# Wide causal attention: k and v projected as two pieces in the third and fourth slot of a unit, and a mask product of 256 columns

## The chip, the cores and the metric

The kernel runs on one core of one Trainium2 chip. The core has a matrix engine (TensorE, in the profile PE, its weight loads PEld), a vector engine (VectorE, DVE), a scalar engine (ScalarE, ACT), GpSimd (POOL) and SyncE (SP), which here issues the transfers. TensorE writes to PSUM, eight banks of 512 float columns; the other operands lie in SBUF. The metric is the device time of one execution in microseconds, as the median of several runs.

## The reference

Four transformer layers on x of 8 sequences x 256 positions x 256 channels. The change touches one of them, the attention of the third layer:

```python
B, T, E = (2, 256, 256)      # the batch is 8 in this case
G, QPG, D = (4, 4, 128)
q = (x @ wq + bq).reshape(b, t, G, QPG, D).transpose(0, 2, 3, 1, 4)
kv = (x @ wkv + bkv).reshape(b, t, G, 1, 2 * D).transpose(0, 2, 3, 1, 4)
k, v = (kv[..., :D], kv[..., D:])
q = q + pe
k = k + pe
scores = jnp.einsum('bgqtd,bgksd->bgqts', q, k) / math.sqrt(D)
causal = jnp.tril(jnp.ones((t, t), dtype=bool))
scores = jnp.where(causal, scores, -jnp.inf)
probs = jax.nn.softmax(scores, axis=-1)
out = jnp.einsum('bgqts,bgksd->btgqd', probs, v).reshape(b, t, G * QPG * D)
return out @ wo
```

x is normalised before it and the result is added to x. pe is a sinusoidal position table. Four heads of a group share one k and one v.

## The kernel before

`four_layers_kernel` runs stages one after the other with a barrier between them: per layer an attention and a feed-forward stage. The function `wide_attention_stage` serves the third layer (`WideAttention(4, 4, shared_kv=True, rope=False, causal=True, ...)`) and the fourth (`rope=True`, not causal). For the fourth, the change alters nothing in what is computed or in its order; the branches with `rope` stay.

All of it works in float32 accuracy from pairs: a number is split into a high part and the rest (low), and each product is made of three passes (high-high, high-low, low-high).

The work is cut into units. A unit is one group of four heads and one sequence, so there are 4 x 8 = 32 units (`over_units`), written out by hand at the edges of a group and as a loop in its middle. A unit has four slots, one for each head (`over_slots`). In slot j of unit u TensorE does, in this order:

- `value` of the head before (L661): out^T = v^T probs^T, 6 products;
- the piece for this slot of the *next* unit: a projection of the normalised x (L583);
- `transposed` of head j (L646): three transposes of the probabilities, after ScalarE's exponentials (`probs_ready`);
- `score` of the next head (L627 and L636): the mask product and six products q^T k;
- `output` of the head before (L583, bank<-w,out_t): six products with wo.

Which slot has which piece stands in `self.pieces` and `self.after` (L306 to L308): q (heads 0 and 1) in slot 0, q2 (heads 2 and 3) in slot 1, kv in slot 2, nothing in slot 3. q and q2 take 12 products of 256 columns each. kv takes 6 of 256 for k and 12 of 128 for v (`bank<-w,z`), and fills one bank: k in its first half, v in its second.

A piece is then read from its bank by VectorE, which adds bias and position (L791, L796) into a buffer `summed`; ScalarE copies that as the high part (L706), and GpSimd subtracts to make the low part (L871, `sum_low`). The scores of the next unit's first head, in slot 3, wait for all three low parts (L620).

Between the transposes of head j and those of head j + 1 the other engines work on the probabilities in turn: ScalarE copies the transposed ones (L732), VectorE subtracts for their low part (L816), then takes the maximum of the next head's scores (L807) and the reciprocal (L829), and ScalarE makes the next exponentials (L724). VectorE and ScalarE take their operations strictly in the order of the program; VectorE's order in a slot is: low part of the output of the head before (L821), the piece's additions, L816, L807, L829, and the addition of the result to x (L835).

The mask is added by TensorE too: before the scores an identity is multiplied with `masks_bf`, 128 x 384 in bfloat16: the triangle for the first 128 queries, zeros for the first half of the second 128 queries' keys, and the triangle for their second half. It opens the bank (`start=True`); the score products accumulate on it. The first 128 queries see 128 keys only, so the scores take 128 + 256 = 384 columns.

Each group has its own weights, in two buffers (high and low). The weights of the next group are split in the slots of the last units of a group (`split_parts_at`, L514): q's in slot 2 and k's and v's in slot 3 of the unit before the last, those of the output in slot 1 of the new group's first unit.

Of the kernel before, what the change touches and what calls it, by code (L numbers as in the profile page):

```python
# [30 lines left out]
P = 128  # L31
# [237 lines left out]
    return slice(t * S, (t + 1) * S)  # L269


def make_masks(nc, masks_bf, mask):

    nc.vector.memset(masks_bf[:, P:2 * P], 0.0)
    nc.vector.tensor_copy(masks_bf[:, 0:P], mask[:])
    return nc.vector.tensor_copy(masks_bf[:, 2 * P:3 * P], mask[:])


class WideAttention:
# [7 lines left out]
    def __init__(self, heads, groups, shared_kv, rope, causal, scale):  # L287
        self.HG, self.G, self.rope, self.causal, self.scale = heads, groups, rope, causal, scale
        self.shared_kv, self.KV = shared_kv, 1 if shared_kv else heads
        widths = [2 * P, heads * P, self.KV * P, self.KV * P] if rope else [heads * P, P, P]  # L290
        scales = [1.0, scale, 1.0, 1.0] if rope else [scale, 1.0, 1.0]
        names = ["rope", "q", "k", "v"] if rope else ["q", "k", "v"]
        at, self.segment, self.parts = 0, {}, []
        for name, width, s in zip(names, widths, scales):
            self.segment[name] = (len(self.parts), at, width)
            self.parts.append((at, at + KT * width, s))
            at += KT * width
        self.wo_at, self.width = at, at + heads * C
        self.parts.append((at, self.width, 1.0))

        if rope:
            self.pieces = [("q", False, ["q"]), ("k", False, ["k"]), ("v", False, ["v"]), ("rope", True, ["rope"])]
            self.before = {0: [0], 1: [2]}
            self.after = {0: [1], 1: [3]}
        else:
            self.pieces = [("q", True, ["q"]), ("q2", True, ["q"]), ("kv", True, ["k", "v"])]  # L306
            self.before = {}
            self.after = {0: [0], 1: [1], 2: [2]}  # L308
        self.ahead = 1 if rope else 0
        self.sums = [i for i, p in enumerate(self.pieces) if p[1]]  # L310


def wide_attention_stage(core, cfg, w_in, consts_in):
# [15 lines left out]
    with Stage(core) as st:  # L329
# [5 lines left out]
        if rope:  # L335
            tables = st.sb("tables", [P, 2, 2 * S])
            consts = [tables]
            turned = st.sb("turned", [P, 2, 2 * S])
            summed = [st.sb("summed", [P, 2 * S]) for _ in range(2)]
            halves = st.sb("halves", [P, 2, 2, S], F32R)  # L340


            q_turned = [st.sb("q_turned", [P, 2, S], F32R) for _ in range(2)]
            k_turned = [[st.sb("k_turned", [P, 2, S], F32R) for _ in range(2)] for _ in range(2)]
            zeroed = st.sem("zeroed")
            moved = [st.sem("moved") for _ in range(2)]
            halves_high, halves_low = st.sem("halves_high"), st.sem("halves_low")
            MOVES = 8
        else:
            position = st.sb("position", [P, S])  # L350
            bias = st.sb("bias", [P, G, HG + 1])
            v_bias = st.sb("v_bias", [P, G, P])
            mask = st.sb("mask", [P, P])
            consts = [position, bias, v_bias, mask]
            scaled_position = st.sb("scaled_position", [P, S])
            scaled_bias = st.sb("scaled_bias", [P, G, HG])
            masks_bf = st.sb("masks_bf", [P, S + P], BF16)
            summed = [st.sb("summed", [P, 2 * S]) for _ in range(2)]
        probs = [st.sb("probs", [P, QT, S]) for _ in range(2)]
        probs_t = [[st.sb("probs_t", [P, NB], F32R) for _ in range(2)] for _ in range(2)]  # L360
# [116 lines left out]
        def destination(u, i, part):  # L477

            name = cfg.pieces[i][0]
            if name == "q":  # L480
                return [(q[u.parity][part][:, 0:2, :], slice(0, 2 * S))]
            if name == "q2":
                return [(q[u.parity][part][:, 2:4, :], slice(0, 2 * S))]
            if name == "k":
                return [(k[u.parity][part][:, 0:2, :], slice(0, 2 * S))]
            if name == "v":
                return [(v[u.parity][part][:], slice(0, 2 * S))]
            return [(k[u.parity][part][:, 0, :], slice(0, S)), (v[u.parity][part][:], slice(S, 2 * S))]

        def shaped(source, target):  # L490
            return source.rearrange("p (a c) -> p a c", a=target.shape[1]) if len(target.shape) == 3 else source
# [13 lines left out]
        def wait_weights_free(eng, g, part):  # L505

            if part < NW - 1:

                last = part if rope else (2 if part == 0 else 3)
                need(eng, piece_done, (g * B - 1) * NP + AHEAD + last)  # L510
            else:
                need(eng, y_done, g * B * HG)

        def split_parts_at(u, j):  # L514

            if not u.in_last_group:
                if u.next().closes:
                    parts = ({0: [0], 1: [1, 2]} if rope else {2: [0], 3: [1, 2]}).get(j, [])
                    return u.g + 1, parts
                if rope and u.closes and j == 0:  # L520
                    return u.g + 1, [3]
            if u.opens and not u.first and j == 1:
                return u.g, [NW - 1]
            return None, []
# [4 lines left out]
        with nc.Block() as block:  # L529
# [40 lines left out]
            def _(pe):  # L570
# [16 lines left out]
                def piece(u, i):  # L587
# [10 lines left out]
                    zz = z[u.parity]  # L598
                    if name != "v":
                        s = segments[0]  # L600
                        for c in range(1 if name == "kv" else 2):
                            first = (c + (2 if name == "q2" else 0)) * P
                            ins = group_of_passes(p[:, c * S:(c + 1) * S], [
                                (lambda a, kt=kt: weights(a, s, kt, first, P), lambda c_, kt=kt: norm_t[c_][:, kt, bass.ds(u.b * S, S)])
                                for kt in range(KT)])
                    if "v" in segments:
                        at = S if name == "kv" else 0
                        for t in range(QT):
                            ins = group_of_passes(p[:, at + t * KV * P:at + (t + 1) * KV * P], [
                                (lambda a, kt=kt: zz[a][:, kt, t * P:(t + 1) * P],  # L610
                                 lambda c_, kt=kt: weights(c_, "v", kt, 0, KV * P)) for kt in range(KT)])
                    ins.then_inc(piece_done, 1)

                def score(u, j):
                    if j == 0:
                        if rope:
                            pe.wait_ge(piece_read, piece_number(u, 1))
                            wait_moved(pe, u)
                        else:
                            pe.wait_ge(sum_low, (u.n + 1) * NS)  # L620
                    if rope and u.first and j == 0:
                        pe.wait_ge(zeroed, 4)
                    need(pe, probs_ready, u.slot(j) - 1)
                    s = s_bank[j % 2]
                    qq, kk, kj = q[u.parity], k[u.parity], 0 if cfg.shared_kv else j
                    if causal:
                        nc.tensor.matmul(s[:, 0:S + P], core.ident_bf[:], masks_bf[:], start=True, stop=False)  # L627
                    for t in range(QT):
                        width = P if causal and t == 0 else S
                        operands = [(qq[a][:, j, t * P:(t + 1) * P], kk[c][:, kj, 0:width])  # L630
# [3 lines left out]
                                         for a, c in ((0, 0), (0, 1), (1, 0))]  # L634
                        for n, (a, c) in enumerate(operands):
                            ins = nc.tensor.matmul(s[:, score_columns(causal, t)], a, c, start=(n == 0 and not causal),  # L636
                                                   stop=(n == len(operands) - 1 and (t == QT - 1 or not causal)))
                    ins.then_inc(scores_done, 1)

                def transposed(u, j):  # L640
# [9 lines left out]
                def value(u, j):  # L650
# [2 lines left out]
                    need(pe, o_low, m)  # L653
                    if j == 0 and rope:
                        pe.wait_ge(piece_read, piece_number(u, 2))
                    jv, vv, pp = 0 if cfg.shared_kv else j, v[u.parity], probs_t[j % 2]
                    for kt in range(QT):
                        to = slice(P, S) if causal and kt else slice(0, S)
# [84 lines left out]
            def _(dve):  # L743
# [23 lines left out]
                def piece(u, i):  # L767
# [17 lines left out]
                        ins.then_inc(piece_read, 1)  # L785
                        return
                    need(dve, sum_low, number - 1)
                    for c in range(1 if name == "kv" else 2):
                        head = c + (2 if name == "q2" else 0)
                        b_ap = bias[:, bass.ds(u.g, 1), HG:HG + 1] if name == "kv" else scaled_bias[:, bass.ds(u.g, 1), head:head + 1]  # L790
                        ins = nc.vector.scalar_tensor_tensor(  # L791
                            target[:, c * S:(c + 1) * S], p[:, c * S:(c + 1) * S], b_ap.rearrange("p a c -> p (a c)"),
                            (position if name == "kv" else scaled_position)[:], ALU.add, ALU.add)
                    if name == "kv":
                        b_ap = v_bias[:, bass.ds(u.g, 1), :].to_broadcast([P, QT, P])
                        ins = nc.vector.tensor_tensor(target[:, S:2 * S].rearrange("p (a c) -> p a c", a=QT),  # L796
                                                      p[:, S:2 * S].rearrange("p (a c) -> p a c", a=QT), b_ap, ALU.add)
                    ins.then_inc(piece_read, 1)

                def score(u, j):  # L800
# [1916 lines left out]
```

## Time and profile before

| | us |
|---|---|
| median of 3 runs | 3215.28 (3204.89 to 3218.27) |
| the profiled execution's own time | 3212.33 |
| its span, first to last instruction | 3210.3 |
| TensorE busy | 2779.6 (87%) |
| VectorE busy | 2066.0 (64%) |
| ScalarE busy | 1601.6 (50%) |
| GpSimd busy | 734.5 (23%) |

The mean granted clock of TensorE over the span is 0.934. The stage that the change touches lies from about 1143 to 1680 us; its first scores start at 1154.09. In a timeline row the columns are start, busy time, engine, line, operation, output and inputs, their shape and the number of instructions merged; a mark in brackets gives the idle time of the engine just before and whose work ended it. Busy times of products overlap, as TensorE is pipelined: what a product costs in a row of them is read from one start to the next.

### The profile page before, as it was taken

The page shows a single profiled execution, that of the slowest core. Times are in us where ns is not written, and L with a number is a line of the kernel's source. Part 1 is how long each engine was busy: PE and PEld are TensorE (multiplying, and loading weights), DVE is VectorE, ACT ScalarE, POOL GpSimd, SP SyncE. Part 2 cuts the span into 40 slices and gives each one's busy share as a digit, 9 for nine tenths or more (in the row PEclk, how much of TensorE's full clock was granted, in tenths as well). Part 3 has the DMA queues.
Part 4 walks back from the last instruction along what each step waited for, and adds up shares of the span by engine and source line. Part 5 has one row for each costly group of instructions (what it writes and reads, how often), then busy time and mean ns, then how long its engine had stood idle before and what let it go on. Part 6 is the DMA issues. An engine that isn't in the chain of part 4 may idle for free. (4 is left out here: it accounts for less than half of the span.)

```text
span 3210.3 us, 67512 instructions
## 1 busy us (share of the span) xinstructions
PE 2779.6 (87%) x20975; PEld 2421.0 (75%) x20979; DVE 2066.0 (64%) x6053; ACT 1601.6 (50%) x4675; POOL 734.5 (23%) x676
## 2 busy tenths in 40 slices
PE   6976999799996579999986879999999996949995
PEld 5755888566665379989984669999999995637774
DVE  5666555677783477777774367777777777425554
ACT  6872333599995155555554444444454444113331
POOL 2110000111100222222224511010101101756663
PEclk9987999899998589999997979999999997969998
DMA  4001111460001020110003533333332325557776
GB/s 127 2 9 35 51 46 51 166 231 2 2 2 41 0 79 27 57 45 33 34 17 135 171 120 94 88 102 100 102 97 86 98 86 216 196 146 122 123 123 163
DMA packets 177282, 274.93 MB, mean 86 GB/s; under 512 B 28016, under 2 KB 145704, under 8 KB 173712
## 3 DMA queue, kind: packets, MB, share of 16 engines
q1 hardware_dynamic: 150352, 228.13, 22.3%
q0 software_dynamic: 26688, 43.80, 6.9%
q8 instruction: 125, 2.05, 0.3%
q14 instruction: 117, 0.96, 0.1%
HBM read 106.97 MB, written 80.98 MB: 59 GB/s over the span
## 5 line engine op out<-in xcount | busy, mean ns | idle before, releaser
L583 PE MATMUL bank<-norm_t_high,w 128*128 128x256 f32 (+1 forms) x2176 | 448.6, 288 | 8.3 <-DVE w L758 8.3
L724 ACT ACTIVATE probs<-bank,neg_max 128x256 f32<-128x256 f32 (+1 forms) x512 | 224.5, 443 | 367.3 <-DVE inv L829 357.6
L583 PEld LDWEIGHTS bank<-norm_t_high,w 128*128 128x128 f32 x2176 | 364.8, 195 | 9.1 <-issue 9.1
L1143 ACT ACTIVATE probs<-neg_scores,bound 128x256 f32<-128x256 f32 (+1 forms) x768 | 367.0, 487 | 2.4 <-DVE bound L1214 1.9
L583 PE MATMUL bank<-norm_t_low,w 128*128 128x256 f32 (+1 forms) x1088 | 310.8, 286 | 0.0
L1214 DVE CUSTOM_DVE_ANT_0 neg_scores<-bank,table 128x256 f32<-128x256 f32 (+1 forms) x768 | 261.8, 397 | 58.6 <-PE bank L1055 58.6
L636 PE MATMUL bank<-k,q 128*128 128x256 f32 (+1 forms) x1536 | 270.8, 299 | 7.5 <-DMA k_turned<-halves 6.3
L732 ACT ACTIVATE probs_t<-bank 128x384 fp32r<-128x384 f32 (+1 forms) x256 | 139.3, 544 | 261.4 <-PE bank L646 260.7
L865 POOL TENSOR_TENSOR summed<-turned 128x512 f32<-128x512 f32 x64 | 82.5, 1289 | 707.1 <-DVE turned L784 707.1
L835 DVE SCALAR_TENSOR_TENSOR x_sb<-bank,inv,x_sb 128x256 f32 (+1 forms) x512 | 224.3, 479 | 24.3 <-DVE inv L829 13.4
L583 PE MATMUL bank<-w,out_t 128*128 128x256 f32 x1536 | 226.7, 283 | 4.3 <-DVE out_t L821 4.1
L2205 POOL DMA_INDIRECT sums<-shared,norm_t x127 | 197.3, 1553 | 132.8 <-ACT shared L2033 128.8
L661 PE MATMUL bank<-probs_t,v 128*128 128x256 f32 (+1 forms) x1536 | 216.8, 277 | 4.5 <-issue 2.9
L636 PEld LDWEIGHTS bank<-k,q 128*128 128x128 f32 x1536 | 212.2, 191 | 11.2 <-issue 9.7
L2018 ACT ACTIVATE acted<-bank 128x176 f32<-128x176 f32 (+2 forms) x222 | 69.5, 313 | 297.9 <-PE bank L1971 218.1
L583 PEld LDWEIGHTS bank<-norm_t_low,w 128*128 128x128 f32 x1088 | 212.0, 195 | 0.0
L1971 PE MATMUL bank<-weights,x_t 128*128 x696 | 208.0, 422 | 3.4 <-issue 1.3
L583 PEld LDWEIGHTS bank<-w,out_t 128*128 128x128 f32 x1536 | 201.7, 190 | 6.6 <-DVE out_t L821 4.4
L661 PEld LDWEIGHTS bank<-probs_t,v 128*128 128x128 f32 x1536 | 200.2, 191 | 6.6 <-DVE probs_t L816 3.5
L1067 PE MATMUL bank<-ident_sb,probs 128*128 128x128 f32 x1408 | 192.7, 278 | 12.8 <-ACT probs_t L1150 12.7
L1067 PEld LDWEIGHTS bank<-ident_sb,probs 128*128 128x128 f32 x1408 | 155.0, 141 | 58.1 <-issue 29.5
L1222 DVE COPY probs_t<-bank 128x512 f32<-128x512 f32 (+1 forms) x192 | 123.5, 643 | 77.7 <-PE bank L1067 76.6
(371 smaller groups left out, 6697.1 us busy)
## 6 DMA issues: line engine op xcount, KB each, us to landing
z<-norm_t_high SPq DMA_DIRECT2D x96, 256.0 KB, 2.5
z<-norm_t_low SPq DMA_DIRECT2D x96, 256.0 KB, 2.5
rows<-blank SPq DMA_DIRECT2D x1, 21336.0 KB, 65.6
norm_t<-rows SPq DMA_DIRECT2D x127, 168.0 KB, 2.9
q_turned<-halves SPq DMA_DIRECT2D x256, 64.0 KB, 2.0
k_turned<-halves SPq DMA_DIRECT2D x256, 64.0 KB, 2.0
staged<-in_attention SPq DMA_DIRECT2D x12, 1280.0 KB, 6.6
staged<-in_experts SPq DMA_DIRECT2D x34, 448.0 KB
```

The costliest lines, as they stand in the source:

```text
L583: ins = nc.tensor.matmul(out, stationary(a), moving(c), start=(kt == 0 and m == 0), stop=(kt == n - 1 and m == 2))
L636: ins = nc.tensor.matmul(s[:, score_columns(causal, t)], a, c, start=(n == 0 and not causal), stop=(n == len(operands) - 1 and (t == QT - ...
L661: ins = nc.tensor.matmul(o_bank[:, to], vv[a][:, kt, jv * P:(jv + 1) * P], pp[c][:, of], start=(kt == 0 and n == 0), stop=(kt == QT - 1 an ...
L724: ins = nc.scalar.activation(probs[j % 2][:, t, 0:width], s_bank[j % 2][:, score_columns(causal, t)], ACT.Exp, bias=neg_max[j % 2][:, t:t ...
L732: nc.scalar.activation(probs_t[j % 2][0][:], t_bank[:, 0:NB], ACT.Copy).then_inc(t_high, 1)
L835: ins = nc.vector.scalar_tensor_tensor(tile, y_bank[j % 2][:, t * C:(t + 1) * C], inv[j % 2][:, t:t + 1], tile, ALU.mult, ALU.add)
L1067: ins = nc.tensor.transpose(t_bank[g % 2][:, at:at + P], probs[q % 2][g][:, t, kt * P:(kt + 1) * P], core.ident[:])
L1143: ins = nc.scalar.activation(probs[q % 2][g][:, t, 0:width], neg_scores[g][:, t, 0:width], ACT.Exp, bias=bound[q % 2][:, g, t:t + 1], scal ...
L1214: ins = nc.vector.tensor_tensor_reduce(out=neg_scores[g][:, t, 0:width], in0=s_bank[g][:, t * S:t * S + width], in1=table[:, at:at + width ...
L1222: nc.vector.tensor_copy(probs_t[q % 2][g][:], t_bank[1][:, 0:NB]).then_inc(t_by_dve, 1)
L1971: ins = nc.tensor.matmul(out, x_t[i.e % 2][:, kt, :], weights[:, kt * i.columns:][:, bass.ds(expert[i.e], i.columns)], start=(kt == 0), st ...
L2205: nc.gpsimd.indirect_dma_start(scratch.results[e % len(scratch.results)], bass.IndirectOffsetOnAxis(ids, 0), product[e % OUT_RING], None, ...
```

## The change

1. The piece kv becomes two pieces, k in slot 2 and v in slot 3. There are four pieces in a unit instead of three (NP and NS), each with its own bank turn, `summed` buffer, semaphore counts and waits. The scores of the next unit's first head wait for the low parts of q, q2 and k alone (`u.n * NS + 3`); a new wait for all four stands before the `value` of each unit's first head.
2. The split of v's weights for the next group moves from slot 3 of the unit before the last to slot 0 of the last unit; k's stays in slot 3.
3. `masks_bf` is 128 x 2 x 128 without the zeros, and the mask product writes columns 0 to 127 and 256 to 383 of the bank. Columns 128 to 255 are first written by the score product of the second 128 queries, which accumulates in a bank that the mask product has opened.

```diff
+def mask_product(nc, core, s, masks_bf):
+    diagonal = s[:].rearrange("p (a c) -> p a c", a=2)[:, :, 0:P]
+    return nc.tensor.matmul(diagonal, core.ident_bf[:], masks_bf[:], start=True, stop=False, skip_group_check=True)
+
 def make_masks(nc, masks_bf, mask):
-    nc.vector.memset(masks_bf[:, P:2 * P], 0.0)
-    nc.vector.tensor_copy(masks_bf[:, 0:P], mask[:])
-    return nc.vector.tensor_copy(masks_bf[:, 2 * P:3 * P], mask[:])
+    nc.vector.tensor_copy(masks_bf[:, 0, :], mask[:])
+    return nc.vector.tensor_copy(masks_bf[:, 1, :], mask[:])
...
-            self.pieces = [("q", True, ["q"]), ("q2", True, ["q"]), ("kv", True, ["k", "v"])]
-            self.after = {0: [0], 1: [1], 2: [2]}
+            self.pieces = [("q", True, ["q"]), ("q2", True, ["q"]), ("k", True, ["k"]), ("v", True, ["v"])]
+            self.after = {0: [0], 1: [1], 2: [2], 3: [3]}
...
-                last = part if rope else (2 if part == 0 else 3)
+                last = part if rope else part + 2
...
-                    parts = ({0: [0], 1: [1, 2]} if rope else {2: [0], 3: [1, 2]}).get(j, [])
+                    parts = ({0: [0], 1: [1, 2]} if rope else {2: [0], 3: [1]}).get(j, [])
                     return u.g + 1, parts
-                if rope and u.closes and j == 0:
-                    return u.g + 1, [3]
+                if u.closes and j == 0:
+                    return u.g + 1, [3 if rope else 2]
...
-                            pe.wait_ge(sum_low, (u.n + 1) * NS)
+                            pe.wait_ge(sum_low, u.n * NS + 3)
...
-                        nc.tensor.matmul(s[:, 0:S + P], core.ident_bf[:], masks_bf[:], start=True, stop=False)
+                        mask_product(nc, core, s, masks_bf)
...
+                    elif j == 0:
+                        pe.wait_ge(sum_low, (u.n + 1) * NS)
```

On TensorE, in slots 2 and 3 of a unit, the rows stand in this order before (`w,z` is v's product, `norm_t_high,w` and `norm_t_low,w` are k's):

```order
L583 MATMUL bank<-norm_t_high,w 128x256
L583 MATMUL bank<-w,z 128x128 x12
L646 MATMUL bank<-ident_sb,probs 128x128 x3
L627 MATMUL bank<-masks_bf,ident_bf 128x384
L636 MATMUL bank<-k,q 128x128 x3
L636 MATMUL bank<-k,q 128x256 x3
L583 MATMUL bank<-w,out_t 128x256 x6
L661 MATMUL bank<-probs_t,v 128x256 x3
L661 MATMUL bank<-probs_t,v 128x128 x3
L646 MATMUL bank<-ident_sb,probs 128x128 x3
```

and with the change:

```order
L587 MATMUL bank<-norm_t_high,w 128x256
L650 MATMUL bank<-ident_sb,probs 128x128 x3
L276 MATMUL bank<-masks_bf,ident_bf 128x2x128
L639 MATMUL bank<-k,q 128x128 x3
L639 MATMUL bank<-k,q 128x256 x3
L587 MATMUL bank<-w,out_t 128x256 x6
L667 MATMUL bank<-probs_t,v 128x256 x3
L667 MATMUL bank<-probs_t,v 128x128 x3
L587 MATMUL bank<-w,z 128x128 x12
L650 MATMUL bank<-ident_sb,probs 128x128 x3
```

v's twelve products have moved from before the first group of transposes to before the second.

On VectorE, the same place before (L791 with `bias` is k's addition, L796 v's):

```order
L821 TENSOR_TENSOR out_t<-bank,out_t 128x256
L791 SCALAR_TENSOR_TENSOR summed<-bank,bias,position 128x256
L796 TENSOR_TENSOR summed<-bank,v_bias 128x256
L816 TENSOR_TENSOR probs_t<-bank,probs_t 128x384
L807 TENSOR_REDUCE neg_max<-bank 128x1 x2
L829 RECIPROCAL inv<-sums 128x2
L835 SCALAR_TENSOR_TENSOR x_sb<-bank,inv,x_sb 128x256 x2
L821 TENSOR_TENSOR out_t<-bank,out_t 128x256
L816 TENSOR_TENSOR probs_t<-bank,probs_t 128x384
```

and with the change:

```order
L831 TENSOR_TENSOR out_t<-bank,out_t 128x256
L799 SCALAR_TENSOR_TENSOR summed<-bank,bias,position 128x256
L826 TENSOR_TENSOR probs_t<-bank,probs_t 128x384
L817 TENSOR_REDUCE neg_max<-bank 128x1 x2
L839 RECIPROCAL inv<-sums 128x2
L845 SCALAR_TENSOR_TENSOR x_sb<-bank,inv,x_sb 128x256 x2
L831 TENSOR_TENSOR out_t<-bank,out_t 128x256
L796 TENSOR_TENSOR summed<-bank,v_bias 128x256
L826 TENSOR_TENSOR probs_t<-bank,probs_t 128x384
```

v's addition has moved one slot on, to the place that the other pieces' additions have in theirs.

## Rows read from the trace of the kernel before

**Rows 1.** Busy time by engine in a window; then clock, DMA share, GB/s.
```profile
1158.00:1674.30 516.30, 488.77 (x4080) 479.07 (x4078) 394.56 (x1084) 281.90 (x898) 123.92 (x124) 1.00 0.11 36
```
**Rows 2.** Waits from 1150 to 1685 us: in total, times, longest.
```profile
PE bank L646 <- ACT probs L724: 21.2, 35, 0.7
```
**Rows 3.** Timeline of TensorE, one unit; columns as above.
```profile
1270.46 0.49 PE L646 MATMUL bank<-ident_sb,probs 128*128 128x128 f32 x3
...
1274.48 0.49 PE L646 MATMUL bank<-ident_sb,probs 128*128 128x128 f32 x3
...
1277.01 0.34 PE L583 MATMUL bank<-norm_t_high,w 128*128 128x256 f32 x1
...
1277.77 1.45 PE L583 MATMUL bank<-w,z 128*128 128x128 f32 x12
1279.06 0.52 PE L646 MATMUL bank<-ident_sb,probs 128*128 128x128 f32 x3
...
1282.37 0.55 PE L646 MATMUL bank<-ident_sb,probs 128*128 128x128 f32 x3 [0.60 <-ACT probs L724]
...
1286.43 0.49 PE L646 MATMUL bank<-ident_sb,probs 128*128 128x128 f32 x3
```
**Rows 4.** Timeline of TensorE and VectorE in the last unit.
```profile
1667.11 0.55 PE L646 MATMUL bank<-ident_sb,probs 128*128 128x128 f32 x3 [0.60 <-ACT probs L724]
...
1670.45 0.55 PE L646 MATMUL bank<-ident_sb,probs 128*128 128x128 f32 x3 [0.59 <-ACT probs L724]
...
1671.56 0.56 DVE L816 TENSOR_TENSOR probs_t<-bank,probs_t 128x384 fp32r<-128x384 f32 x1 [0.43 <-ACT probs_t L732]
```
**Rows 5.** Timeline of all engines between two groups of transposes.
```profile
1279.44 0.98 PE L636 MATMUL bank<-k,q 128*128 128x128 f32 x6
...
1280.13 0.56 DVE L816 TENSOR_TENSOR probs_t<-bank,probs_t 128x384 fp32r<-128x384 f32 x1
...
1280.61 0.61 DVE L807 TENSOR_REDUCE neg_max<-bank 128x1 f32<-128x128 f32 x2
...
1280.99 0.74 POOL L871 TENSOR_TENSOR k<-summed,k 128x256 fp32r<-128x256 f32 x1 [3.33 <-ACT v L706]
...
1282.12 0.20 ACT L724 ACTIVATION_READ_ACCUMULATOR probs<-bank,neg_max 128x1 f32 x1
1282.21 0.38 ACT L737 ACTIVATE out_t<-bank 128x256 fp32r<-128x256 f32 x1
```
**Rows 6.** Weight loads behind a mask product: two windows, from 1274.82 and 1275.1.
```profile
1274.81 0.46 PEld L636 LDWEIGHTS bank<-k,q 128*128 128x128 f32 x3
...
1274.97 0.41 PEld L636 LDWEIGHTS bank<-k,q 128*128 128x128 f32 x3
```
**Rows 7.** Timeline where the next group's weights are split.
```profile
1260.58 1.05 ACT L686 ACTIVATE w<-staged 128x1024 fp32r<-128x1024 f32 x1
...
1262.04 0.51 PE L646 MATMUL bank<-ident_sb,probs 128*128 128x128 f32 x3
...
1263.54 0.42 DVE L796 TENSOR_TENSOR summed<-bank,v_bias 128x256 f32<-128x256 f32 x1
1263.87 0.55 DVE L816 TENSOR_TENSOR probs_t<-bank,probs_t 128x384 fp32r<-128x384 f32 x1
...
1266.10 0.55 PE L646 MATMUL bank<-ident_sb,probs 128*128 128x128 f32 x3 [0.72 <-ACT probs L724]
```
**Rows 8.** Timeline of a group's first unit, slot 2 of it.
```profile
1290.46 0.49 PE L646 MATMUL bank<-ident_sb,probs 128*128 128x128 f32 x3
...
1296.44 0.51 PE L646 MATMUL bank<-ident_sb,probs 128*128 128x128 f32 x3
```
**Rows 9.** Timeline of the stage's start.
```profile
1150.59 1.26 POOL L871 TENSOR_TENSOR q<-summed,q 128x512 fp32r<-128x512 f32 x1 [0.79 <-ACT q L706]
...
1154.09 0.34 PE L627 MATMUL bank<-masks_bf,ident_bf 128*128 128x384 bf16 x1 [3.15 <-POOL v L871]
```
**Rows 10.** Timeline of TensorE, the stage's one stop with no releaser.
```profile
1417.54 1.29 PE L661 MATMUL bank<-probs_t,v 128*128 128x256 f32 x6 [2.88 <-issue]
```

More of the change, by code:

```diff
@@ L356, in wide_attention_stage @@
             scaled_bias = st.sb("scaled_bias", [P, G, HG])
-            masks_bf = st.sb("masks_bf", [P, S + P], BF16)
+            masks_bf = st.sb("masks_bf", [P, 2, P], BF16)
             summed = [st.sb("summed", [P, 2 * S]) for _ in range(2)]
@@ L484, in destination @@
             if name == "k":
[L485 to L488, printed above, removed]
+                return [(k[u.parity][part][:], slice(0, KV * S))]
+            return [(v[u.parity][part][:], slice(0, KV * S))]
         def shaped(source, target):
@@ L600, in piece @@
                         s = segments[0]
-                        for c in range(1 if name == "kv" else 2):
+                        for c in range(KV if name == "k" else 2):
                             first = (c + (2 if name == "q2" else 0)) * P
@@ L606, in piece @@
                     if "v" in segments:
-                        at = S if name == "kv" else 0
                         for t in range(QT):
-                            ins = group_of_passes(p[:, at + t * KV * P:at + (t + 1) * KV * P], [
+                            ins = group_of_passes(p[:, t * KV * P:(t + 1) * KV * P], [
                                 (lambda a, kt=kt: zz[a][:, kt, t * P:(t + 1) * P],
@@ L636, in score @@
                             ins = nc.tensor.matmul(s[:, score_columns(causal, t)], a, c, start=(n == 0 and not causal),
-                                                   stop=(n == len(operands) - 1 and (t == QT - 1 or not causal)))
+                                                   stop=(n == len(operands) - 1 and (t == QT - 1 or not causal)),
+                                                   skip_group_check=causal)
                     ins.then_inc(scores_done, 1)
@@ L787, in piece @@
                     need(dve, sum_low, number - 1)
-                    for c in range(1 if name == "kv" else 2):
-                        head = c + (2 if name == "q2" else 0)
-                        b_ap = bias[:, bass.ds(u.g, 1), HG:HG + 1] if name == "kv" else scaled_bias[:, bass.ds(u.g, 1), head:head + 1]
-                        ins = nc.vector.scalar_tensor_tensor(
[L792 to L797, printed above, removed]
+                    if name == "v":
+                        b_ap = v_bias[:, bass.ds(u.g, 1), :].to_broadcast([P, QT, P])
+                        ins = nc.vector.tensor_tensor(target[:, 0:S].rearrange("p (a c) -> p a c", a=QT),
+                                                      p[:, 0:S].rearrange("p (a c) -> p a c", a=QT), b_ap, ALU.add)
+                    elif name == "k":
+                        ins = nc.vector.scalar_tensor_tensor(
+                            target[:, 0:S], p[:, 0:S], bias[:, bass.ds(u.g, 1), HG:HG + 1].rearrange("p a c -> p (a c)"), position[:], ALU.add, ALU.add)
+                    else:
+                        for c in range(2):
+                            head = c + (2 if name == "q2" else 0)
+                            b_ap = scaled_bias[:, bass.ds(u.g, 1), head:head + 1]
+                            ins = nc.vector.scalar_tensor_tensor(
+                                target[:, c * S:(c + 1) * S], p[:, c * S:(c + 1) * S], b_ap.rearrange("p a c -> p (a c)"), scaled_position[:],
+                                ALU.add, ALU.add)
                     ins.then_inc(piece_read, 1)
```

## The prediction

> **What bounds the kernel now.** I read the page first (the table above): its busy shares are means over many stages, and the change touches one of them. So the next view is the table of windows for that stage, the wide causal attention of the third layer (1158 to 1674.3 us). There TensorE is busy 488.77 of 516.30 us at a granted clock of 1.00, the upper of its two levels, 2.4 GHz; VectorE is busy 394.56 us and nobody else comes near [rows 1]. So TensorE is the bound, with 27.5 us in which it is idle. The list of waits says where: 21.2 us in 35 pieces are transposes (L646) that wait for ScalarE's exponentials (L724) [rows 2]. 35 is nearly one for each of the 32 units.
>
> The timeline of TensorE in one unit shows which slot waits. I measure a slot from the first transpose of a head to that of the next [rows 3]. Slot A (from 1270.46) holds the product of piece q2 and lasts 4.02 us; B (from 1274.48) holds kv and lasts 4.58; C (from 1279.06) holds no piece and lasts 3.31; D (from 1282.37) holds the next unit's q and lasts 4.06. The sum is 15.97. Only C's end carries the idle mark (0.60 us, on the exponentials).
>
> What ends C is a chain through three engines, seen in the timeline of all engines [rows 5]: transposes at 1279.06, ScalarE's copy of them, VectorE's subtraction 1280.13, the maximum of the next head's scores 1280.61, exponentials read out by 1282.12 + 0.20, and the next transposes at 1282.37, 0.05 later. That is 3.31 us whatever TensorE does in between. The last unit, which has no pieces at all, runs every slot on this chain: 1667.11 to 1670.45 is 3.34 [rows 4]. So a slot costs the larger of TensorE's own work and about 3.31 to 3.34.
>
> **The change part by part.**
>
> 1. Slot B loses v's product. v's 12 products of 128 columns stand from 1277.77 to the transposes at 1279.06, which is 1.29 us (0.108 each) [rows 3]. TensorE's work in B falls from 4.58 to 3.29, or 3.24 with the smaller mask product (point 3). That is now just under the chain, so the chain ends B: 3.31. Gain 1.27. TensorE then idles under 0.1 us here; the cover for a longer chain is gone in this slot.
>
> 2. Slot C gains v's product. What a slot holds beside its piece is read from B: 1274.48 to 1277.01, 2.53 us [rows 3]. C becomes 2.53 + 1.29, less 0.05 for the mask, plus about 0.03 because v now follows other 128-column products: 3.80. That is 0.5 over the chain, so the 0.60 idle goes and nothing waits in its place. Loss 0.49.
>
> 3. The mask product goes from 384 to 256 columns, 128 times. Its price is not its duration but how long it holds up the next weight load. The first load behind it starts at 1274.81, and three loads are still seen from 1274.97 on [rows 6]: a gap of 0.16 us, where 128-column products follow one another every 0.108 and 256-column ones every 0.12 (six of them from 1277.01 to 1277.77, with a start of 0.17) [rows 3]. 256 columns of the mask should cost 0.11. Gain 0.05 in each slot that TensorE bounds (A, C, D), nothing in B, where the chain decides. Bounds: 0 if the gapped target (two runs of 128 columns) costs what was saved, 0.06 at best. I take 0.05. No row shows a product with such a target.
>
> 4. D begins after a stop now and runs 0.04 longer than A, the time in which the loads start up again. Without the stop, D is 4.02 and with the mask 3.97: gain 0.09. A: 4.02 to 3.97, gain 0.05.
>
> In one unit: 1.27 - 0.49 + 0.09 + 0.05 = 0.92. Pieces are made in 31 of the 32 units: 31 x 0.92 = 28.5 us.
>
> The Trainium skill (TensorE: Matmul & The Clock Gate, Back-to-back issue gap) gives about 81 ns for sustained 128-column products with their weight loads; the trace disagrees with 108 [rows 3]. By the page v's product would be 0.97 and C 3.48, and the gain 31 x 0.32 = 9.9 us larger. The trace is of this very product, so the sum keeps 1.29.
>
> 5. Work of the other engines: the number and size of VectorE's, ScalarE's and GpSimd's operations is the same, half of what stood in slot B moves on to C. In B and C VectorE has the same order (piece, subtraction, maximum), and both slots' ends now have what slots A and D have already: one piece between value and transpose. At B's end the chain runs through q2's additions, as it does before; at C's end it is longer at most by VectorE's k addition, under 0.5 us of cover.
>
> 6. Waits that are new. The scores of the next unit's first head (in C) now wait for q, q2 and k only, and the values of that head, one slot later, for v. k's rest on GpSimd starts 1.93 us after the transposes that open C and takes 0.74 [rows 5]; with v no longer in front of it on ScalarE it ends no later than 2.7. The scores stand behind v's product and three transposes, 3.80 + 0.33 after the same point. 1.4 us are left. v's rest has a whole slot more. Behind those scores stand the output and value products, on which everything waits, so if this were late it would count in full; it isn't by these rows. SP's loads of the inputs of v wait for the pieces of two units back, as before, and v reads them a slot later: more room.
>
> 7. Where a group of heads ends, weights are split. Once in each of three groups the split of q's 1024 columns (ScalarE, 1.05 us from 1260.58) makes slot C 4.06 instead of 3.31 (1262.04 to 1266.10) [rows 7]. Here the chain decides, and it starts at the split, 5.52 us before 1266.10; v's product hid its first 1.46 us. In the change slot C opens 0.16 after the operation that follows the exponentials on ScalarE (1282.21 to 1282.37) [rows 5], which here is the split. So C is 5.52 - 0.16, less 0.33 for v's addition (1263.54 to 1263.87), which leaves VectorE's queue there: 5.03. B + C was 4.59 + 4.06 (B by the trace of this unit as in the others) and becomes 3.31 + 5.03; D, with one small split fewer, falls from 4.36 (1266.10 to 1270.46) to 3.97 [rows 3, 7]; the unit gains 0.31 + 0.39 + 0.05 = 0.75 instead of 0.92: 3 x -0.17 = -0.5. In the first unit of three groups slot B lasts 5.98 (1290.46 to 1296.44) [rows 8], for the split of the output weights; it loses v's 1.29 and the mask's 0.05 and would be 4.64, but the split lies on the chain too, so I take 4.8, a gain of 1.2 instead of 1.27: -0.2.
>
> 8. The stage's start. TensorE's first scores stood idle for 3.15 us until 1154.09, for GpSimd's rests of q2 (1.26 from 1150.59), k and v [rows 9]. Now k can follow q2 at once at 1151.85, ends 0.74 later at 1152.6, and v is not waited for: 1.5 us earlier. Bounds 0.7 (v's operation alone, as long as k's) and the whole 3.15.
>
> Sum: 28.5 - 0.5 - 0.2 + 1.5 = 29.3 us. Against the profiled execution's own time, 3212.33 us, that gives 3183.0; the median of the runs shown is 3 us above the profiled one, so I predict 3184.
>
> **Rivals.**
> - The filled slot is right, but the mask product saves nothing (the gapped target costs what the columns save): 3 x 31 x 0.05 = 4.7 less, 3189. For it: no such product in the trace. Against: the array takes the same stream of columns.
> - Slot B's chain is longer than read, since what B was hiding (output and value products, VectorE's reads of x) now runs close behind it. 3.31 and 3.34 are the two readings; if VectorE's addition of k came on top (at 0.33, as v's in [rows 7]), B would be 3.64: 31 x 0.33 = 10 less, 3194. Against: VectorE's subtraction started 1.07 after the transposes where kv's additions stood before it (1280.13), and 1.11 in the last unit, where none did (1671.56) [rows 4, 5].
> - The gap comes back as stalls of another kind. Once, before 1417.54, TensorE stands 2.88 us for nothing that the profile shows, and its six products behind it take 1.29 [rows 10], where six steps of 0.12 and an end would be 0.8: some 3.4 us in all. The loops' code changes in length; one such stall more in each of eight turns of a loop gives 3184 + 27 = 3211, no change.
> - Slower than before: the mask product with two runs of 128 columns. If such a target kept the next weight load from starting before the product has ended, each would cost the full duration of a short product, 0.27 us (three transposes take 0.49, less two steps of 0.11), and a load step of 0.11 [rows 3]: 0.38. Slots A, C and D pay it whole, B only what is over the 0.2 us by which the scores' end (1279.44 + 0.98) lies ahead of their maximum (1280.61) [rows 5]. It decides from 0.28 us each; at 0.38 it costs 96 x 0.38 + 32 x 0.18 = 42 us and the 4.7 saved: 3231. For it only that no row shows such a target. Against: the stream into the array is one of 256 columns either way, and the steps of 0.12 in [rows 3] are the same whichever part of a bank a product writes.
>
> **How the numbers follow.** Forecast 0.80 (its own range 3175 to 3193, from 0 or 0.06 for the mask, 0.7 or 3.15 at the start, and the 13 us between the runs shown); mask saves nothing 0.07; longer chain 0.05; stalls 0.05; gapped target 0.03. The range reaches over the first two rivals: 3172 to 3198. A difference of 0.5% is 16 us: faster 0.92, same 0.05, slower 0.03.
>
> **What the profile would show.** The transposes' wait for the exponentials falls from 21.2 us to a few, in pieces under 0.1 us, and stands at the end of slot B. Slots of one unit read 3.97, 3.31, 3.80, 3.97 and sum to 15.05. The weight load behind the mask product starts 0.11 after the one before. The stage takes about 29 us less and everything behind it starts as much earlier with unchanged lengths. I am wrong if B stays above 3.5, if C shows an idle mark, or if the scores wait for GpSimd's k inside the units.

## The result, and the profile after

| | before | with the change |
|---|---|---|
| median, us | 3216.23 (6 runs) | 3192.65 (3183.33 to 3196.18, 6 runs) |
| the profiled execution, us | 3212.33 | 3183.33 |
| ratio, 95% interval | | 0.9922 [0.9904, 0.9939] |
| steady unit: slots A, B, C, D; the unit (medians) | 4.00, 4.58, 3.31, 4.06; 15.96 | 3.98, 3.29, 3.88, 3.99; 15.13 |

By the medians the change makes the kernel 23.6 us faster. On a second chip, on which the kernel before took 3299.55 us, it took 3272.07 us, a ratio of 0.9917 [0.9904, 0.9929]. The profiled execution with the change is the fastest of its six. A steady unit is one that lies at no edge of a group of heads, where weights are split.

The first view is again the timeline of TensorE in one unit, with the change:

```profile
1261.64 0.49 PE L650 MATMUL bank<-ident_sb,probs 128*128 128x128 f32 x3
...
1265.59 0.49 PE L650 MATMUL bank<-ident_sb,probs 128*128 128x128 f32 x3
...
1268.88 0.55 PE L650 MATMUL bank<-ident_sb,probs 128*128 128x128 f32 x3
...
1271.42 1.50 PE L587 MATMUL bank<-w,z 128*128 128x128 f32 x12
1272.76 0.51 PE L650 MATMUL bank<-ident_sb,probs 128*128 128x128 f32 x3
...
1276.74 0.49 PE L650 MATMUL bank<-ident_sb,probs 128*128 128x128 f32 x3
```

Against [rows 3]: B has fallen from 4.58 to 3.29, and it is now B's end that is on the chain through ScalarE and VectorE, as the experiments below show. Its mark in the timeline is small: the transposes at 1268.88 take 0.55 instead of 0.49, as those behind a stop do in [rows 4]. v's product stands in C (1271.42 to 1272.76, 1.34 us), where the 0.60 us of idle stood.

The list of waits from 1140 to 1660 us, against [rows 2]:

```profile
PE bank L650 <- ACT probs L730: 2.9, 5, 0.7
...
PE bank L276 <- POOL k L881: 1.1, 1, 1.1
```

21.2 us of waiting for the exponentials have become 2.9. The five that are left are the stage's first transposes (0.23) and the four slots that hold no piece, one in the last unit but one and three in the last (0.65 to 0.66 each); none stands at a B, whose stops are too short for this list. The wait of the first scores, 3.15 us in [rows 9], is 1.15 in the timeline. The table of windows, from 1.2 us behind the first transposes ([rows 1]: 0.6) to the last:

```profile
1155.40:1647.50 492.10, 480.16 (x4073) 471.59 (x4071) 394.79 (x1082) 281.75 (x897) 125.91 (x124) 1.00 0.11 38
```

TensorE is busy for 480.16 of 492.10 us, where in [rows 1] it was 488.77 of 516.30. The idle time went from 27.5 to 11.9 us, and busy time, which overlaps between products, fell by 8.6.

The two profiled executions differ by 28.8 us of span. The stage itself is 25.8 of it: 2.2 from its start to the first transposes, 23.6 from the first to the last of them. The rest lies in other stages, which vary by themselves: in the twelve profiled executions the second stage (its first row of L171) began between 221.7 and 234.1 us, in code that is the same in all.

### The profile page after: what moved, and what is told of

Read it like the earlier page. It is cut to its first block and busy times, and to the rows that moved or that the text cites. A ratio compares the mean times of both kernels' runs of the same rounds, so it can differ in the third digit from the quotient of the medians.

```text
span 3181.5 us, 67532 instructions
## 1 busy us (share of the span) xinstructions
PE 2766.9 (87%) x20975; PEld 2410.9 (76%) x20979; DVE 2067.8 (65%) x6052; ACT 1602.8 (50%) x4675; POOL 737.6 (23%) x676
## 5 line engine op out<-in xcount | busy, mean ns | idle before, releaser
L639 PE MATMUL bank<-k,q 128*128 128x256 f32 (+1 forms) x1536 | 264.4, 295 | 8.7 <-DMA k_turned<-halves 6.9
L639 PEld LDWEIGHTS bank<-k,q 128*128 128x128 f32 x1536 | 205.7, 191 | 12.8 <-issue 10.0
```

## The experiments

The slots below are medians of steady units, read from each run's trace. The runs stand on three chips; the kernel before took 3299.55 us (17 runs) on the one of the mask product alone, the pieces alone, the change itself and the first run with late splits, 3303.80 (one run) on that of the longer chain, the gapless target, the single pass and k last, and 3217.47 (9 runs) on that of the operation behind the subtraction and of all splits late.

**The mask product alone.** The kernel before with `mask_product`, kv in one piece.

> The kernel before with the mask product of 256 columns alone; kv stays one piece. My theory (the product holds up the next weight load by 0.16 us, now 0.11, and this counts only where TensorE bounds the slot): slots A, B and D each 0.05 shorter (3.96, 4.53, 4.01), C unchanged at 3.31 with its stop, 31 x 0.15 = 4.7 us in all, ratio 0.9985. Rival 'the gapped target costs what the columns save': all slots as before, ratio 1.000. Rival 'duration counts everywhere': C shorter too.

Measured: slots 3.96, 4.53, 3.32, 4.02, unit 15.81 instead of 15.96; ratio 0.9988 [0.9978, 0.9998]. As my theory had it: 0.05 in A, B and D, nothing in C, which is on the chain.

**The pieces alone.**

```diff
-                        mask_product(nc, core, s, masks_bf)
+                        nc.tensor.matmul(s[:, 0:S + P], core.ident_bf[:], masks_bf[:], start=True, stop=False)
```

> The change with the old mask product of 384 columns. My theory: slots A 4.02, B 3.30 (on the chain, so the same as in the change), C 3.93, D 4.04; that is 0.15 a unit or some 5 us more than the change, 20 us less than before, ratio 0.9935 to 0.9945. If slot B were bound by TensorE's work it would be 3.35 here, 0.05 over the change.

Measured: 4.01, 3.29, 3.93, 4.03, unit 15.26; ratio 0.9936 [0.9924, 0.9949]. B is the same with either mask, so the chain ends it. The pieces are 0.70 of the 0.83 us that a steady unit gains, the mask 0.13.

**The change itself on that chip.**

> The change itself on the chip of these runs, as the measure for the others. Ratio 0.992; slots A 3.96, B 3.30, C 3.88, D 3.99, sum 15.11.

Measured: 3.98, 3.29, 3.88, 3.99; ratio 0.9917 [0.9904, 0.9929].

**A gapless target for the mask product.**

```diff
-    diagonal = s[:].rearrange("p (a c) -> p a c", a=2)[:, :, 0:P]
-    return nc.tensor.matmul(diagonal, core.ident_bf[:], masks_bf[:], start=True, stop=False, skip_group_check=True)
+    return nc.tensor.matmul(s[:, 0:2 * P], core.ident_bf[:], masks_bf[:].rearrange("p a c -> p (a c)"), start=True, ...
```

> The change with the mask product's 256 columns written to columns 0 to 255 of the bank without a gap, instead of 0 to 127 and 256 to 383 (so the second 128 queries get their mask in the wrong half). If a gapped target costs nothing, slots are as in the change (3.96, 3.30, 3.88, 3.99) and the product's duration stays 0.27. If it costs, A, C and D are shorter here.

Measured: 3.98, 3.30, 3.87, 3.99, all within 0.003 of the change, and the product's duration is 0.27 in both; 3277.31 us in one run. Two runs of 128 columns cost nothing here.

**v's product in one pass.**

> The change with v's product in its first pass only (4 of 12 products; the two passes with the low parts are left out). My theory (slot C = 2.5 us of other work and 12 steps of 0.11): C would be 3.88 - 0.89 = 2.99 by TensorE's work, so the chain ends it at 3.30 and the stop for the exponentials is back in both B and C; A and D unchanged, D starting after a stop 0.04 longer; a unit 14.55, 17 us less than the change. Rival 'C is bound by something else than v's product': C stays near 3.88.

Measured: 3.99, 3.30, 3.35, 4.01, unit 14.65; 3262.88 us in one run. In the list of waits from 1165 to 1640 us the wait for the exponentials is back:

```profile
PE bank L655 <- ACT probs L735: 9.0, 34, 0.7
```

C fell by 0.53 and not by v's 0.89, since the chain catches it at 3.35. So v's product is what lifts C over the chain, and 0.5 us is all that a shorter one could give there.

**k last.** The two pieces exchanged, with the splits of their weights moved to fit. The new wait for all four low parts now stands before the scores, and the one before the value product of a unit's first head is gone.

```diff
-            self.pieces = [..., ("k", True, ["k"]), ("v", True, ["v"])]
+            self.pieces = [..., ("v", True, ["v"]), ("k", True, ["k"])]
...
-                            pe.wait_ge(sum_low, u.n * NS + 3)
+                            pe.wait_ge(sum_low, (u.n + 1) * NS)
```

> The change with the two new pieces exchanged: v in the third slot and k in the fourth, and the scores of the next unit's first head wait for all four low parts (the splits of k's and v's weights both lie in the last unit's first slot). By rows, k's low part is ready about 2.3 us after the transposes that follow k's product, and the scores come 0.3 after them: TensorE stands 1.8 to 2.1 us in each unit. Slot B holds v (3.90), C holds k, about 3.3; D, in which scores now wait, grows from 3.99 to 5.5 to 6. Unit 16.7 to 17.2, 45 to 65 us more than the change, and more than before by 20 to 40. If the wait were not on the path (rival: the low part is early), the unit stays at 15.1.

Measured: 3.96, 3.82, 3.32, 6.03, unit 17.13; 3352.46 us in one run, 48.7 more than the kernel before and 75 more than the gapless run, where 20 to 40 and 45 to 65 were expected. The timeline, in slot D:

```profile
1304.01 0.55 PE L650 MATMUL bank<-ident_sb,probs 128*128 128x128 f32 x3
...
1305.67 0.72 POOL L879 TENSOR_TENSOR k<-summed,k 128x256 fp32r<-128x256 f32 x1 [2.82 <-ACT k L710]
...
1306.45 0.28 PE L276 MATMUL bank<-masks_bf,ident_bf 128*128 128x256 bf16 x1 [1.89 <-POOL k L879]
```

k's way through VectorE, ScalarE and GpSimd takes 2.4 us from the transposes (1304.01 to 1306.39); TensorE stands 1.89 us for it. What the expectation left out is the clock: in nine of the 31 units D took 7.5 to 7.6 instead of 6.0, as after the stop the granted clock fell to the lower of its two levels (1.2 GHz) for part of the slot. In one of them it was 0.62 on the mean from 1196.4 to 1200.7 us, and the six score products took 1.63 instead of 0.94; behind the stops in the slots of 6.0 it stayed at 1.00. The same two pieces in this order lose, so it is the order, k first, that makes the split pay. The run also gives v's product in a slot that does not begin after a stop: B 3.82.

**A longer chain.** One operation more on VectorE.

```diff
                     dve.wait_ge(t_high, u.slot(j) + 1)
+                    if causal:
+                        nc.vector.tensor_scalar(scratch[:], position[:, 0:P], 1.0, None, ALU.mult)
```

> The change with one operation more on VectorE in each slot (128 x 128, into a scratch tile), between the wait for ScalarE's copy and VectorE's subtraction for the low part, so that the chain between two groups of transposes is longer by its step d (some 0.15 to 0.3 us). My theory (the chain of 3.30 ends slot B, TensorE's work ends A, C and D with 0.6 to 0.7 us to spare): B grows by all of d, A, C and D by nothing; the last unit's four slots grow by d too. Rival 'TensorE's work of 3.24 ends B and the chain has slack': B grows by less than d by as much as the slack.

Measured: 4.11, 3.43, 3.94, 4.09; 3279.57 us in one run. B and the last unit's slots grew alike, by 0.13, as expected; the operation moved the subtraction by 0.15 (1310.98 to 1311.13 below). A, C and D grew too, by 0.14, 0.06 and 0.10, which my theory excluded. The timeline of slot A shows the place:

```profile
1309.86 0.49 PE L651 MATMUL bank<-ident_sb,probs 128*128 128x128 f32 x3
...
1310.98 0.88 PE L588 MATMUL bank<-w,out_t 128*128 128x256 f32 x6
1310.98 0.23 DVE L828 TENSOR_SCALAR scratch<-position 128x128 f32<-128x128 f32 x1
...
1311.13 0.55 DVE L829 TENSOR_TENSOR probs_t<-bank,probs_t 128x384 fp32r<-128x384 f32 x1
...
1311.81 0.90 PE L668 MATMUL bank<-probs_t,v 128*128 128x256 f32 x6
```

The value product should follow the output product by 0.71 (1311.69) and starts at 1311.81, just after VectorE's subtraction ends at 1311.68. There is a second chain: transposes, ScalarE's copy, VectorE's subtraction, value product.

**The same operation behind the subtraction**, to tell the second chain from a VectorE without room.

> The change with the same additional VectorE operation as in the run with the longer chain, but right behind VectorE's subtraction instead of ahead of it. There A, C and D grew too (0.13, 0.06, 0.10), against my theory. New theory: a second chain, transposes, ScalarE's copy, VectorE's subtraction, value product, has only some 0.05 us to spare in those slots. Here the subtraction is not delayed and only the exponentials are: B and the last unit's slots grow by 0.13, A, C and D by nothing (3.97, 3.88, 3.99). Rival (VectorE is simply too busy in those slots, or the chain of the exponentials has no room in them): A, C and D grow as there.

Measured: 4.20, 3.43, 3.88, 3.98; 3205.50 us in one run. C and D stand as in the change, so it is the subtraction's time that counted there, and B grows by 0.13. A failed: it grew by 0.22. The timeline of a steady slot D, and of A behind it from 1339.23, shows a cost of this experiment's own:

```profile
1336.67 0.73 POOL L884 TENSOR_TENSOR v<-summed,v 128x256 fp32r<-128x256 f32 x1 [2.90 <-ACT v L713]
1336.79 0.69 DVE L830 TENSOR_SCALAR scratch<-position 128x128 f32<-128x128 f32 x1
...
1339.23 0.49 PE L651 MATMUL bank<-ident_sb,probs 128*128 128x128 f32 x3
...
1339.74 0.87 DVE L806 SCALAR_TENSOR_TENSOR summed<-bank,scaled_bias,scaled_position 128x256 f32<-128x256 f32 x2
...
1340.53 0.54 DVE L827 TENSOR_TENSOR probs_t<-bank,probs_t 128x384 fp32r<-128x384 f32 x1
...
1341.21 0.90 PE L668 MATMUL bank<-probs_t,v 128*128 128x256 f32 x6
```

Beside GpSimd's subtraction for v the added operation takes 0.69 instead of 0.22 us (28 of 128 do), so D's exponentials come late and VectorE begins A late: q2's additions start 0.51 after the transposes (in the change 0.29, from 1293.46 to 1293.75), the subtraction 1.30 after them (1.09), and the value product 1.98 (1.84), 0.14 after the subtraction's end. So the subtraction was late in A after all, and the second chain can account for this growth too. That is read from the rows; for A no run separates the two.

**Splits late.** In the change, ScalarE's part of the split of q, k and v weights goes behind its copy of the transposed probabilities, VectorE's part to the start of the next slot.

```diff
                     nc.scalar.activation(probs_t[j % 2][0][:], t_bank[:, 0:NB], ACT.Copy).then_inc(t_high, 1)
+                    if not rope:
+                        split_high(*split_parts_at(u, j, late=False))
...
                 def slot_start(u, j):
+                    if not rope:
+                        split_low(*split_parts_at(u, j, late=True))
```

> The change with the splits of q's, k's and v's weights for the next group moved: ScalarE makes the high part in the middle of a slot, behind its copy of the transposed probabilities, and VectorE the low part at the start of the slot after. The split of the output weights stays. My theory (in slot C of the unit before a group's last, q's split lies in series on the chain, 1.05 and 1.23 us, which makes C 5.48): both parts now lie mostly in gaps of their engines, C falls from 5.48 to 4.0 to 4.4 and D grows from 3.99 to 4.0 to 4.4 for VectorE's part: 0.7 to 1.4 us in each of three groups, 2 to 4 us, ratio to before 0.991. Rival 'the split costs its length wherever it is': C + D stay at 9.47.

Measured: C in that unit 3.88 and D 3.99, as if there were no split: 1.6 us in each of three groups, more than the 0.7 to 1.4 expected. 3268.07 us, ratio 0.9906 [0.9893, 0.9919], which cannot be told from the change's in time.

**All splits late.** The output weights' too, in slots 0 and 1 of a group's first unit.

> The kernel with q's, k's and v's splits late, and the split of the output weights likewise: ScalarE's part in the middle of a group's first slot, VectorE's at the start of the second. My theory: the first slot B of a group falls from 4.82 to about 3.9 to 4.1, as ScalarE's 1.05 us leaves that slot's chain and fits before the first slot's exponentials (0.7 us to spare); A grows by at most 0.4. 1.5 to 3 us over three groups, ratio to before 0.990. Rival: VectorE's part (1.23 us) and the output product's wait for it set the slot, B stays over 4.5.

Measured: in the first such unit B falls from 4.83 to 3.61, more than expected, and A grows from 4.03 to 4.54, more than the 0.4 expected; over the three groups B gains 3.3 us and A loses 1.5 against the run before. 3182.27 us, ratio 0.9889 [0.9869, 0.9909]. From first to last transposes it is 6.3 us shorter than the change (486.45 against 492.75) and 0.6 shorter than the run before (487.07). Its ratio is the lowest of the versions that do all of the work, but the intervals of the two overlap: that the output weights' late split gains in time is not shown.

## Why the prediction was right, and where it was off

The forecast was 29.3 us for the stage and 3184 for the median; the stage gained 25.8 and the median is 3192.65, inside the range of 3172 to 3198. By its own working (3183.0 and 3 us more) the median should have been forecast at 3186. That the profiled execution took 3183.33 where the sum said 3183.0 is luck: the stage fell 3.5 us short, other stages were 3 us shorter by themselves, and this execution was the fastest of six.

By the slots, the 3.5 us are roughly 2.4 less in C, 1.1 less at the splits and 1.2 less in A and D, against 0.7 more at the start and 0.3 more in B.

1. **Slot B (point 1): right.** 3.31 forecast, 3.29 measured. That the chain ends it is shown by the pieces alone (the same B with 0.05 more work on TensorE) and by the longer chain (B grows as the last unit's slots do).
2. **Slot C (point 2): the mechanism right, the size 0.08 short**, 3.80 forecast and 3.88 measured, 2.4 us over 31 units. Two parts. v's 12 products took 1.34 where they took 1.29 in B; 0.03 of this was forecast, 0.02 was not. And point 4 said that D's restart after a stop would be gone; it only moved: B ends in a stop now, and C pays the restart, some 0.06. With no stop ahead, in the run with k last, v's slot is 3.82.
3. **The mask (point 3): right**, 0.05 in three slots, none in the slot on the chain. The two rivals that priced the gapped target are refuted by the gapless run.
4. **Slots A and D (point 4):** 3.97 and 3.97 forecast, 3.98 and 3.99 measured. A is less even than before: from 3.95 to 4.05 in steady units, and 4.18 and 4.20 in two of the groups' last, where the kernel before had 4.00 to 4.03. With k last, a version without the new wait before the first head's value product, steady units have 3.95 to 3.97. So the wait is a suspect, but no run adds it alone.
5. **Room (points 2 and 5): the step that failed.** "That is 0.5 over the chain, so the 0.60 idle goes and nothing waits in its place" held in time, but it follows the exponentials' chain alone, and that was not the only one. A second, through VectorE's subtraction to the value product, has under 0.15 us of room in A, C and D: a subtraction 0.15 later made them 0.14, 0.06 and 0.10 longer.
6. **The new wait (point 6): right.** In the change k's low part is ready 2.35 us after the transposes that open C (2.7 at most was forecast) and the scores come at 4.23. With k last the same 2.4 us became a stop of 1.89.
7. **Splits of weights (point 7): the sign right, the size wrong.** C in the unit before a group's last was forecast at 5.03 and is 5.48; -1.6 us over three groups instead of -0.5. The step that failed counted only the exponentials' chain. The timeline of all engines there:

```profile
1252.01 1.05 ACT L692 ACTIVATE w<-staged 128x1024 fp32r<-128x1024 f32 x1
...
1253.09 1.23 DVE L764 SCALAR_TENSOR_TENSOR w<-staged,w 128x1024 fp32r<-128x1024 f32 x1 [1.10 <-ACT w L692]
...
1254.23 0.42 DVE L831 TENSOR_TENSOR out_t<-bank,out_t 128x256 fp32r<-128x256 f32 x1
...
1254.71 0.97 PE L587 MATMUL bank<-w,out_t 128*128 128x256 f32 x6 [1.20 <-DVE out_t L831]
...
1254.96 0.55 DVE L826 TENSOR_TENSOR probs_t<-bank,probs_t 128x384 fp32r<-128x384 f32 x1
...
1256.94 0.20 ACT L730 ACTIVATION_READ_ACCUMULATOR probs<-bank,neg_max 128x1 f32 x1
```

   The exponentials are read out at 1257.14, near the forecast. But the output product had waited 1.20 us for VectorE's low part of the output, which stands behind the split, and then output, value and v's product run until 1257.65. With the split out of the way the whole 1.6 us is gone. That it is the output product's wait that counts, and not the exponentials', is read from these rows: the run moved the whole split and does not part the two. In a group's first unit B was forecast at 4.8 and is 4.64 to 4.83.
8. **The start (point 8): right in its mechanism, the size 0.7 short.** 1.5 forecast, 2.2 measured. The wait shrank by 2.0 (3.15 to 1.15), and it is now GpSimd's k that ends it.

Of the rivals, a longer chain in B and more stalls did not come: B is 3.29, and there is still one stop with no releaser in the slots (D of the unit before the loop's turn lasts 8.06, before it lasted 8.73). The rival priced one such stop at 3.4 us; by the slot it costs 4.7 (8.73 against 4.06).

## What to carry to other kernels

When a slot of a pipeline waits on a chain and its neighbour holds too much, moving work over is worth at most the smaller of the idle time filled and the excess over the chain (here some 0.7 in C and 1.3 in B, and the pieces alone brought 0.70); read both slots and the chain's own length from a slot that has nothing else in it. Follow every wait of the queue that will be short of room, not only the one that ends the slot: here the value and the output product each wait for VectorE on their own. Of pieces that go through several engines, the one that is needed first goes first.

## What the runs showed of the hardware

A TensorE product whose target is two runs of 128 columns with a gap took the same time as one without (0.27 us, slots equal within 0.003).

A VectorE operation with one input and its output in SBUF took 0.22 us alone and 0.69 when a GpSimd subtraction of 0.73 had started before it: it started at 1336.79, GpSimd ended at 1337.40, it at 1337.48. All 28 long ones of that run started after GpSimd's. In 35 other cases it was VectorE that started first; it took 0.22, and GpSimd's subtraction for k, 0.73 otherwise, up to 0.80. The Trainium skill (SBUF — State Buffer, Who interferes with whom) says that `tensor_scalar` in a two-port mode and GpSimd shut each other out for a whole instruction; the trace agrees with the shutting out, and no run shows the mode. The kernel's own VectorE operations that run beside GpSimd's in this stage show no such lengthening: the subtraction for the probabilities, which reads PSUM and SBUF, takes 0.56 with and without.

A stop of TensorE can cost more than its length: after stops of 1.89 us the granted clock fell to the lower level in nine of 31 units, and their slots took 7.5 to 7.6 us instead of 6.0 (run with k last).
